# Value tiles between the units of the first head's maxima in a two-layer decoder kernel

## The chip, the cores and the metric

The kernel runs on one core of a Trainium2 chip. The metric is the device time of one execution in microseconds, and smaller is better. The core has five engines that run their own instruction lists and wait for each other by semaphores: TensorE (PE in the profile; its weight loads are PEld), VectorE (DVE), ScalarE (ACT), GpSimd (POOL) and SyncE (SP, which only issues DMAs).

## What is computed

Two decoder layers on x of 2048 tokens by 256, each layer a self attention, a cross attention over a context of 1601 tokens, and a feed-forward part (an fp8 matmul in the first layer; an MLP inside the second self attention and a mixture of experts after it). Every attention has 16 heads of 16 columns. The part that matters here, cut from the reference:

```python
def attention(x, ctx, Wq, Wk, Wv, Wo, ...):      # the same form four times
    q, k, v = split_heads(x @ Wq.T + bq), split_heads(ctx @ Wk.T + bk), split_heads(ctx @ Wv.T + bv)
    scores = einsum('bhqd,bhkd->bhqk', q, k) / sqrt(16)
    scores = where(mask, scores, -inf)           # causal, given mask, causal, none
    attn = softmax(scores, axis=-1)
    return einsum('bhqk,bhkd->bhqd', attn, v).reshape(...) @ Wo.T + bo

x = layernorm(x + attention(x, x, ...))          # layer 0, with rope: the first attention
x = layernorm(x + attention(x, ctx_1024, ...))   # the second
...
x = layernorm(x + self_attention_and_mlp(x))     # layer 1: the third
x = layernorm(x + attention(x, ctx_1024, ...))   # the fourth
```

## The kernel before

The program is a row of phases; `attention_phase` (line 124) is called four times, for the first self attention, the first cross attention, the second self attention and the second cross attention. In the text these are the first to fourth attention. All work in it is written by hand in order, one list per engine, and the order of a list is the order of execution. Nothing is scheduled by a planner.

A phase begins with a front. There TensorE makes two kinds of tiles, in the order of the list `front`:

- **cut tiles** (L477 transposes, L481 products): the queries and keys of 8 heads by up to 512 tokens in fp32. ScalarE (L405, L411) and VectorE (L643 or L646, L653) cut each into three bf16 parts, and SyncE and GpSimd store the parts in HBM in turn (L229). There are 16 cut tiles in each attention.
- **value tiles** (L471): 128 tokens by 256 columns, two fp32 matmuls each, 16 of them in a self attention and 13 in a cross attention (the last has 65 tokens). ScalarE copies each into `values` (L426, raises `v_kept`), and in the second to fourth attention GpSimd adds the bias (L354). The memory of `values` is called `vall` in the profile.

Both kinds go in turn through four PSUM banks, 3 to 6 (`front_bank`). `made(kind, i)` waits until the tile four places earlier has been read.

SyncE loads the parts of a head's queries and keys back as a **stack** of 96 rows (L253 and L254, 12 loads a head), the one of head 0 while the last cut tiles are still being made. VectorE sets some constants behind the cuts (memsets, L746 to L751) and waits for them.

Then come the **maxima**: the softmax needs the maximum of each query's scores. A **unit** (`unit(h, u)`) is one piece of the scores of head h with the queries as rows: 128 queries by up to 512 keys in a self attention, four matmuls side by side (L496), with four more that add the causal mask on the diagonal (L500); by 401 or 398 keys in a cross attention. A self attention has 40 units a head, a cross attention 64. Units go in turn through three PSUM banks, 0 to 2 (`M_BANKS`), and VectorE reduces each to a column (L669, in the second attention L665). With all units of a head reduced, VectorE makes the head's maximum in six small steps (`finish_max`, L677 to L692), which stand between the first six units of the next head, SyncE stores it and loads it back into the stack as three more rows (`place_max`, L263 and L266).

TensorE's list is: all of `front`, the units of head 0, the first `early_units` of head 1, then for each head the scores with the keys as rows (`scores`, L520, with the masks L525 or L528), ScalarE's exponentials of them (L434), and their products with the values (`product`, L548). The units of the next heads are mixed in between. The first `scores(0, 0)` waits for the loaded maxima (`max_in`), for `v_kept` of all value tiles, and where there is a bias for `v_shifted` of all of them.

The order of the front, as it is written:

```python
for kind, i in front:
    if loads and (kind, i) == front[len(work) if work[0][0][0] is None else 0]:
        pe.wait_ge(loaded, 16 * len(loads))
    made(kind, i)
for u in range(nu):
    unit(0, u)
for u in range(early_units):
    unit(1, u)
```

## Time and profile before

| | |
|---|---|
| median of 3 runs | 3324.24 us (3316.51 to 3329.48) |
| the profiled execution | 3327.38 us, of which the span is 3325.6 us |
| TensorE busy | 90% |
| VectorE busy | 71% |
| ScalarE busy | 51% |
| GpSimd busy | 15% |
| mean granted clock of TensorE | 0.936 |

The span runs from the first to the last instruction of the profiled execution. Times of a row are counted from its start. A granted clock of 1.00 is 2.4 GHz, one of 0.50 is 1.2 GHz; a number between them over a window is a mean of the two. In a timeline a row may merge several instructions of a line: its second number is the time from the first one's start to the last one's end. The brackets at a row's end give the idle time ahead of it, and what ended it.

### The profile page before, as it was taken

How to read it: one execution, taken by the hardware profiler on the slowest of the kernel's cores; microseconds unless marked ns; L12 is line 12 of the kernel's file. 1: busy time of each engine (PE TensorE's matmuls, PEld its weight loads, DVE VectorE, ACT ScalarE, POOL GpSimd, SP SyncE). 2: the span in 40 equal slices, each digit the busy share in tenths (PEclk: the TensorE clock that was granted, in tenths of full speed). 3: DMA queues.
4: the chain of work that ended last, by engine and by line, in shares of the span. 5: the costliest groups of instructions: out<-in, count | busy, mean ns of one | idle time of the engine just before them, and what ended most of it. 6: DMA issues, size and time to landing. Idle time of an engine off the chain costs nothing. (4 is left out here: it accounts for less than half of the span.)

```text
span 3325.6 us, 96922 instructions
## 1 busy us (share of the span) xinstructions
PE 2983.0 (90%) x41211; PEld 1713.7 (52%) x41211; DVE 2348.1 (71%) x5743; ACT 1708.3 (51%) x2162; POOL 497.9 (15%) x558
## 2 busy tenths in 40 slices
PE   3199999889999999994699999898999999989996
PEld 1146666554556656653346665465333333356663
DVE  5888888558777777746788887215999999733114
ACT  1146666643565555561347777413377777731221
POOL 3335555011000000000122211001100000001113
PEclk8579999997999999997789999999799999989998
DMA  2134333230011100010311111103011221121112
GB/s 63 50 95 112 107 112 106 63 100 14 21 23 24 23 23 18 21 32 16 100 28 44 38 38 35 49 0 115 25 37 49 71 49 43 30 63 56 46 44 81
DMA packets 127271, 171.79 MB, mean 52 GB/s; under 512 B 45719, under 2 KB 97879, under 8 KB 124983
## 3 DMA queue, kind: packets, MB, share of 16 engines
q1 hardware_dynamic: 116040, 118.83, 13.8%
q0 software_dynamic: 10800, 46.76, 4.4%
q8 instruction: 326, 5.34, 0.7%
q14 instruction: 105, 0.86, 0.1%
HBM read 122.50 MB, written 35.13 MB: 47 GB/s over the span
## 5 line engine op out<-in xcount | busy, mean ns | idle before, releaser
L669 DVE TENSOR_REDUCE mpart<-ps 128x1 f32<-128x512 f32 (+5 forms) x2304 | 1245.4, 589 | 142.9 <-PE ps L496 78.2
L496 PE MATMUL ps<-stack 96*32 96x401 bf16 (+5 forms) x13312 | 1266.7, 355 | 22.2 <-DVE mpart L669 18.0
L520 PE MATMUL ps<-stack 99*32 99x512 bf16 (+3 forms) x11648 | 1137.0, 369 | 40.9 <-ACT xT L434 19.8
L434 ACT ACTIVATE xT<-ps 128x1024 f32<-128x1024 f32 (+3 forms) x800 | 732.2, 938 | 444.4 <-PE ps L520 237.0
L434 ACT ACTIVATE cn<-ps 128x1024 f32<-128x1024 f32 (+4 forms) x800 | 686.8, 870 | 337.2 <-PE ps L520 176.8
L496 PEld LDWEIGHTS ps<-stack 96*32 96x32 bf16 x13312 | 496.6, 96 | 511.7 <-DVE mpart L669 250.2
L665 DVE CUSTOM_DVE_ANT_0 scrap<-ps,arena 128x401 bf16<-128x401 f32 (+1 forms) x1024 | 550.3, 574 | 150.0 <-PE ps L496 125.5
L520 PEld LDWEIGHTS ps<-stack 99*32 99x32 bf16 x11648 | 417.2, 97 | 358.6 <-issue 122.4
L548 PE MATMUL ps<-xT,vall 128*17 128x512 f32 (+4 forms) x3648 | 455.9, 506 | 0.1
L548 PE MATMUL ps<-cn,vall 128*17 128x512 f32 (+3 forms) x3392 | 441.7, 496 | 0.9 <-ACT cn L434 0.5
L528 PE MATMUL ps<-arena,big 128*32 128x512 fp8e4 (+1 forms) x3264 | 360.7, 381 | 0.0
L500 PE MATMUL ps<-upper,ident 128*32 128x128 bf16 x2048 | 216.3, 227 | 0.0
L548 PEld LDWEIGHTS ps<-xT,vall 128*17 128x17 f32 (+1 forms) x3648 | 134.0, 98 | 47.1 <-issue 2.5
L528 PEld LDWEIGHTS ps<-arena,big 128*32 128x32 bf16 (+1 forms) x3264 | 123.7, 98 | 52.6 <-issue 5.0
L548 PEld LDWEIGHTS ps<-cn,vall 128*17 128x17 f32 (+1 forms) x3392 | 126.9, 98 | 43.5 <-ACT cn L434 3.2
L1287 PE MATMUL ps<-arena,vall 128*128 x312 | 146.6, 593 | 0.6 <-ACT vall L1358 0.6
L1517 DVE TENSOR_TENSOR vall<-osb,ps 128x512 f32<-128x512 f32 x39 | 26.8, 687 | 146.2 <-PE ps L1287 146.2
L525 PE MATMUL ps<-lower,ident 128*32 128x128 bf16 x1024 | 122.3, 223 | 0.0
L500 PEld LDWEIGHTS ps<-upper,ident 128*32 128x32 bf16 x2048 | 105.5, 100 | 24.6 <-issue 1.1
L1017 POOL PARTITION_ALL_REDUCE small<-small x1 | 0.4, 371 | 743.3 <-issue 743.3
L1372 ACT ACTIVATE osb<-ps 128x512 f32<-128x512 f32 x39 | 23.3, 598 | 169.8 <-PE ps L1287 169.8
L371 POOL TENSOR_SCALAR arena<-wbuf 128x1601 bf16<-128x1601 int32 x16 | 90.2, 5640 | 81.6 <-DMA wbuf<-in_mask 81.6
(235 smaller groups left out, 2646.4 us busy)
## 6 DMA issues: line engine op xcount, KB each, us to landing
stack<-q_parts SPq DMA_DIRECT2D x384, 64.0 KB, 2.6
wbuf<-in_mask POOLq DMA_DIRECT2D x16, 800.5 KB, 5.5
stack<-k_parts SPq DMA_DIRECT2D x192, 64.0 KB, 2.7
wbuf<-in_maskT POOLq DMA_DIRECT2D x12, 1024.0 KB, 5.4
arena<-in_moe_w SPq DMA_DIRECT2D x19, 512.0 KB, 4.5
stack<-k_parts SPq DMA_DIRECT2D x192, 50.0 KB, 2.3
parts<-osb SPq DMA_DIRECT2D x240, 32.0 KB
q_parts<-parts SPq DMA_DIRECT2D x16, 384.0 KB, 3.1
```

What stands on the lines that cost most here:

```text
L371: chain.link(nc.gpsimd.tensor_scalar(e.mask_add[:, t, :], given[:, 0:S2], 0.0, MASKED, ALU.is_equal, ALU.mult))
L434: nc.scalar.activation(e.prob[tile % P_SLOTS][0:rows, half * HALF + first:(half + 1) * HALF], S_PS(g)[0:rows, first:HALF], ACT.Exp, scale= ...
L496: last = nc.tensor.matmul(bank[quarter(j), 0:w], qs[b][0:KQ, t * P + 32 * j:t * P + 32 * j + 32], ks[b][0:KQ, a:a + w], start=True, stop=n ...
L500: last = nc.tensor.matmul(bank[quarter(j), w - P:w], e.ident16[:, quarter(j)], e.upper16, start=False, stop=True)
L520: last = nc.tensor.matmul(S_PS(g)[quarter(j), lo:hi], ks[b][0:KM, kt * P + 32 * j:kt * P + 32 * j + 32], qs[b][0:KM, half * HALF + lo:half ...
L525: last = nc.tensor.matmul(S_PS(g)[quarter(j), lo:lo + P], e.ident16[:, quarter(j)], e.lower16, start=False, stop=True)
L528: last = nc.tensor.matmul(S_PS(g)[quarter(j), lo:hi], e.big16[0:rows, quarter(j)], e.mask_one[0:rows, kt, half * HALF + lo:half * HALF + h ...
L548: last = nc.tensor.matmul(O_PS[quarter(j, HD + 1), b0 * P:CH], e.values[0:rows, kt, h, :], weights[0:rows, b0:4, j, :], start=(kt == 0), s ...
L665: nc.vector.tensor_tensor_reduce(out=e.scrap[:, g % 4, 0:w], in0=src, in1=e.mask_add[:, t, a:a + w], scale=1.0, scalar=-3.0e38, op0=ALU.ad ...
L669: nc.vector.tensor_reduce(dst, src, AX, ALU.max).then_inc(unit_used, 1)
L1287: last = nc.tensor.matmul(bank, e.pair_xT[i % 2][:, c, :], w, start=(c == 0), stop=(c == NC - 1))
L1517: nc.vector.tensor_tensor(e.pair_h[i % 2], e.gated_s[i % 2], b_bank(i), ALU.mult).then_inc(pair_h, 1)
```

## The change

The loop over `front` on TensorE is split. The cut tiles are made first, as before. The value tiles are no longer made behind them: one is made behind every second or third unit of head 0 in a self attention (16 among 40 units) and behind every fourth or fifth in a cross attention (13 among 64). The last one stands behind the last unit. The wait for the loaded weights (`loads`, in the first attention alone) stays ahead of the first unit.

```diff
-                for kind, i in front:
-                    if loads and (kind, i) == front[len(work) if work[0][0][0] is None else 0]:
-                        pe.wait_ge(loaded, 16 * len(loads))
-                    made(kind, i)
+                turned_front = work[0][0][0] is None
+                if loads and not turned_front:
+                    pe.wait_ge(loaded, 16 * len(loads))
+                for i in range(len(work)):
+                    made("cut", i)
+                if loads and turned_front:
+                    pe.wait_ge(loaded, 16 * len(loads))
+                valued = 0
                 for u in range(nu):
                     unit(0, u)
+                    while valued < nk * (u + 1) // nu:
+                        made("value", valued)
+                        valued += 1
                 for u in range(early_units):
                     unit(1, u)
```

Only TensorE's list changes. The lists of the other four engines are the same, instruction by instruction. Each value tile is two rows of L471 in the list; `x2` counts them.

TensorE in the first attention, from the last cut transposes to unit 4, before. The names: `ps` is PSUM, `arena` holds the queries and keys, `wbuf` the value weights, `xT` the turned x, `stack_304` the stack of head 0, `upper` the causal mask.

```order
L477 MATMUL ps<-ident,arena 128x128 x64
L471 MATMUL ps<-wbuf,xT 128x256 x32
L496 MATMUL ps<-stack_304 32x128 x4
L500 MATMUL ps<-upper,ident 32x128 x4
L496 MATMUL ps<-stack_304 32x256 x4
L500 MATMUL ps<-upper,ident 32x128 x4
L496 MATMUL ps<-stack_304 32x384 x4
L500 MATMUL ps<-upper,ident 32x128 x4
L496 MATMUL ps<-stack_304 32x512 x4
L500 MATMUL ps<-upper,ident 32x128 x4
```

The same place after the change:

```order
L477 MATMUL ps<-ident,arena 128x128 x64
L496 MATMUL ps<-stack_304 32x128 x4
L500 MATMUL ps<-upper,ident 32x128 x4
L496 MATMUL ps<-stack_304 32x256 x4
L500 MATMUL ps<-upper,ident 32x128 x4
L496 MATMUL ps<-stack_304 32x384 x4
L500 MATMUL ps<-upper,ident 32x128 x4
L471 MATMUL ps<-wbuf,xT 128x256 x2
L496 MATMUL ps<-stack_304 32x512 x4
L500 MATMUL ps<-upper,ident 32x128 x4
```

The 32 matmuls of the 16 value tiles are gone from behind the transposes; the first tile stands behind unit 2.

TensorE in the second attention, from the last cut tiles to the first units, before. Here `cn` holds the turned context, which the value tiles and the keys are made from, and a unit is 32x401 x4 or 32x398 x4.

```order
L481 MATMUL ps<-cn,wbuf 128x512 x6
L481 MATMUL ps<-cn,wbuf 128x65 x2
L471 MATMUL ps<-wbuf,cn 128x256 x24
L471 MATMUL ps<-wbuf,cn 65x256 x2
L496 MATMUL ps<-stack_13673 32x401 x12
L496 MATMUL ps<-stack_13673 32x398 x4
```

After the change:

```order
L481 MATMUL ps<-cn,wbuf 128x512 x6
L481 MATMUL ps<-cn,wbuf 128x65 x2
L496 MATMUL ps<-stack_13673 32x401 x12
L496 MATMUL ps<-stack_13673 32x398 x4
L496 MATMUL ps<-stack_13673 32x401 x4
L471 MATMUL ps<-wbuf,cn 128x256 x2
L496 MATMUL ps<-stack_13673 32x401 x8
L496 MATMUL ps<-stack_13673 32x398 x4
L496 MATMUL ps<-stack_13673 32x401 x8
L471 MATMUL ps<-wbuf,cn 128x256 x2
```

The tiles stand five units apart, and no longer between the last cut tile and unit 0.

## Rows read from the trace of the kernel before

**Rows 1.** The page, part 1: busy time, share of the span, instructions.

```profile
PE 2983.0 (90%) x41211; PEld 1713.7 (52%) x41211; DVE 2348.1 (71%) x5743; ACT 1708.3 (51%) x2162; POOL 497.9 (15%) x558
```

**Rows 2.** Timeline, TensorE, first attention: start us, us, engine, line, operation, count.

```profile
172.88 11.56 PE L471 MATMUL ps<-wbuf,xT 128*128 128x256 f32 x52 [1.17 <-DVE parts L643]
185.47 0.70 PE L496 MATMUL ps<-stack 96*32 96x512 bf16 x8
```

**Rows 3.** Timeline, VectorE, first attention.

```profile
181.57 0.48 DVE L751 MEMSET ps<- 128x512 f32 x1
184.79 20.84 DVE L669 TENSOR_REDUCE mpart<-ps 128x1 f32<-128x128 f32 x40 [2.73 <-PE ps L500]
205.67 0.22 DVE L677 TENSOR_REDUCE mfin<-mpart 128x16 f32<-128x64 f32 x1
```

**Rows 4.** Timeline, SyncE's queue and TensorE, first attention; the page, part 6.

```profile
171.88 0.43 SPq L254 DMA_DIRECT2D stack<-q_parts  x1
...
213.19 0.62 PE L520 MATMUL ps<-stack 99*32 99x512 bf16 x4 [0.82 <-DMA stack<-max_parts]
...
stack<-q_parts SPq DMA_DIRECT2D x384, 64.0 KB, 2.6
```

**Rows 5.** Windows: us, TensorE busy (count), granted clock, DMA share, GB/s.

```profile
190.00:192.00 2.00, 1.50 (x20) 0.74 0.00 0
728.00:735.20 7.20, 4.77 (x20) 1.00 0.82 245
746.00:748.00 2.00, 1.45 (x18) 0.84 0.57 116
```

**Rows 6.** Timeline, TensorE and VectorE, second attention.

```profile
743.99 0.70 PE L496 MATMUL ps<-stack 96*32 96x401 bf16 x12
745.16 0.35 PE L496 MATMUL ps<-stack 96*32 96x398 bf16 x4 [0.47 <-DVE mpart L665]
...
742.15 0.48 DVE L751 MEMSET ps<- 128x512 f32 x1
744.52 0.58 DVE L665 CUSTOM_DVE_ANT_0 scrap<-ps,arena 128x401 bf16<-128x401 f32 x1 [1.89 <-PE ps L496]
745.02 0.57 DVE L665 CUSTOM_DVE_ANT_0 scrap<-ps,arena 128x401 bf16<-128x401 f32 x1
...
776.31 0.22 DVE L677 TENSOR_REDUCE mfin<-mpart 128x16 f32<-128x64 f32 x1
```

**Rows 7.** Timeline, VectorE, third attention.

```profile
1657.38 0.48 DVE L751 MEMSET ps<- 128x512 f32 x1
1660.61 20.84 DVE L669 TENSOR_REDUCE mpart<-ps 128x1 f32<-128x128 f32 x40 [2.74 <-PE ps L500]
1681.49 0.22 DVE L677 TENSOR_REDUCE mfin<-mpart 128x16 f32<-128x64 f32 x1
```

**Rows 8.** Timeline, VectorE, fourth attention.

```profile
2324.36 0.48 DVE L751 MEMSET ps<- 128x512 f32 x1
2326.69 30.89 DVE L669 TENSOR_REDUCE mpart<-ps 128x1 f32<-128x401 f32 x64 [1.85 <-PE ps L496]
2357.62 0.22 DVE L677 TENSOR_REDUCE mfin<-mpart 128x16 f32<-128x64 f32 x1
```

**Rows 9.** Windows behind the first scores of the four attentions.

```profile
213.20:221.70 8.50, 8.23 (x88) 0.50 0.31 83
785.30:788.30 3.00, 3.00 (x36) 0.50 0.44 101
1688.80:1696.20 7.40, 7.11 (x64) 0.50 0.36 97
2368.80:2375.50 6.70, 6.43 (x60) 0.50 0.14 35
```

**Rows 10.** Timeline and window, TensorE, first cut tiles of the second attention.

```profile
702.12 9.22 PE L481 MATMUL ps<-xT,wbuf 128*128 128x512 f32 x16 [1.04 <-PEq L240]
...
706.00:708.00 2.00, 2.00 (x5) 0.90 0.00 0
```

## The prediction

> **What bounds the kernel now.** I read the page first: TensorE is busy 90% of the span [rows 1], so outside a few stages whatever delays TensorE delays the end. The diff touches one stage, which occurs four times, once in each attention phase: the value tiles and the maxima of head 0. So I read TensorE's and VectorE's timelines of these four stretches, then the granted clock in them, then what the first scores wait for.
>
> In the first attention the 16 value tiles run on TensorE without a gap until the first unit starts. The row of 52 products gives the price of a tile: the first 51 take 11.56 less the last one's 0.38, so 11.18 / 51 = 0.22 us each at the full clock, and a tile has four in the trace (two matmuls, each recorded as two), 0.87 us [rows 2]. VectorE ends its memsets at 181.57 + 0.48 = 182.05 and idles 2.73 us for the first unit. Then it reduces 40 units in 20.84 us and goes on at 205.67 with the final maximum of head 0 [rows 3]. In this stretch VectorE is the bound and TensorE waits for banks. After it come the final maximum, two copies by SyncE and the first scores, which wait on the copy of the maxima with 0.82 us of idle TensorE [rows 4]. **So the end of VectorE's head 0 is on the path**, and what it moves by, the first scores move by; from there TensorE is dense, and I expect no later stage to give the shift back. The third attention has the same form (1657.86, 1660.61, 1681.49) [rows 7]. The cross attentions have 64 units: memsets end at 742.63, first unit 744.52, head 0 ends 776.31 [rows 6]; and 2324.84, 2326.69, 2357.62 [rows 8].
>
> **Part 1: the value tiles leave the place ahead of unit 0.** Removed there: 58 tiles (16 + 13 + 16 + 13) of 0.87 us. Not all of that was on the path, since VectorE's memsets ran beside them. What VectorE can win is the idle time between its last memset and its first reduction: 2.7, 1.9, 2.7 and 1.9 us, together 9.2 us. For this the stack of head 0 must have arrived by 182.05: its last load was issued at 171.88 and a load of this size lands in 2.6 us [rows 4], so near 175, with 7 us to spare. Units 0 to 2 then stand in their banks when VectorE is ready. After its last cut TensorE now waits for the stack, does three units, and waits again for VectorE: it is nearly idle for 8 to 13 us where it was dense.
>
> **Part 2: the tiles now stand between the units.** The cost is TensorE time in a stretch that VectorE bounded. Constants from the rows: a unit takes TensorE its width at 2.4 GHz, 0.21 us for 512 columns and 0.17 for 401; the rows agree, with two of the one and three of the other in 0.70 us, the last one's way to the bank included [rows 2, 6]. VectorE's pitch is 0.60 for 512, 20.84 / 40 = 0.52 in the mean, 0.50 for the masked 401 (744.52 to 745.02) and 30.89 / 64 = 0.48 for the unmasked [rows 3, 6, 8]. After VectorE is done with a bank TensorE restarts 0.15 us later (745.02 to 745.16) and VectorE gets a unit 0.36 us after its last column has entered (743.99 + 0.17 to 744.52) [rows 6]. The weight load of a tile I cost at nothing, since TensorE's loads run ahead; uncovered at each of the 58 tiles it would be about 0.1 us, so up to 5.8 us, which I keep for the upper end.
>
> Self attention (first and third): 40 units have 17408 columns and 2048 more for the diagonals. Without the first three units 18304 are left, at 2.4 GHz 7.6 us, and 15 tiles of 0.87 are 13.0. That makes 20.6 us of TensorE, with 0.35 before it (first reduction 0.20, restart 0.15), and 0.36 and 0.60 behind it until VectorE is done: 21.9 us. VectorE alone needs 20.9. **TensorE becomes the bound by a little.** Narrow early units do not cover a tile; I put 0.5 us on that.
>
> Cross attention: VectorE needs 31.7 us (second) and 30.9 (fourth). A tile lies between two units in a ring of three banks. From the release of a bank to the next but one unit in VectorE's hands it takes 0.15 + 0.17 + 0.87 + 0.17 + 0.36 = 1.72 us; three reductions cover 1.49 or 1.45. So each of 12 tiles (the 13th stands behind the last unit) costs 0.23 or 0.27: 2.8 and 3.2 us.
>
> **Part 3: the clock.** The granted clock falls from 1.00 to 0.50 (2.4 to 1.2 GHz) in the unit stage of before: the mean of 0.74 over 190 to 192 puts it near 191, 6.6 us after the last value tile, and in the second attention near 747.4, 3.4 us after it [rows 5]. It is then low until 2.9 to 8.5 us after the first scores [rows 9]. Changed, TensorE comes to the interleaved stretch out of a nearly idle time, so I take it to start there at 1.2 GHz. How long? In the second attention's cuts TensorE starts dense at 702.12 and the clock is back near 706.4 (0.90 over 706 to 708): 4.3 us [rows 10]. At half clock TensorE is behind in all four stages and therefore dense, so I take 4.3. In a self attention this loses half of it, 2.1 us. In a cross attention a group of five units and a tile at 1.2 GHz takes 1.73 for the tile, 0.33 + 0.36 + 0.50 + 0.15 until the fourth unit may start, 0.50 and 0.33 for the fourth and fifth: 3.9 us, against 2.7 at full clock; 4.3 us hold 1.1 such groups, so 1.3 us.
>
> The Trainium skill ("TensorE: Matmul & The Clock Gate", section "HAM oscillation — how this bites in real kernels") says that idle stretches between bursts send TensorE back to half rate; that speaks against this change, which puts such a stretch right ahead of TensorE's heaviest work. If the clock were full at once, as the plain reading of the 1.00 in the value stage of before would have it, the sum below would be 6.8 us lower.
>
> **The sum.** First attention: 182.05 + 21.9 + 0.5 + 2.1 = 206.55, was 205.67: +0.9. Third: the same, +0.9. Second: 742.63 + 31.7 + 2.8 + 1.3 = 778.4, was 776.3: +2.1. Fourth: 2324.84 + 30.9 + 3.2 + 1.3 = 2360.2, was 2357.6: +2.6. Together **+6.5 us**. ScalarE and GpSimd keep their orders: the value copies and the bias additions only come later, the last of them some 1.5 us after head 0 ends, while the first scores follow 7.5 us after it in the first attention (205.67 to 213.19). GpSimd's additions now lie beside the reductions; they did so in the third attention already, where 40 reductions took the same 20.84 us as in the first, which has none [rows 3, 7]. So both cost nothing. The profiled execution took 3327.4 us (span 3325.6), the median is 3324.2. By the first the sum is 3334, by the median 3331; I give 3331.
>
> **Rivals.**
> The clock stays at 2.4 GHz beyond the values (faster). The tiles keep TensorE fuller up to the end of head 0, and the first scores might then start at full clock. Before, the first scores ran 8.5, 3.0, 7.4 and 6.7 us at 0.50 [rows 9]: 25.6 us, of which half, 12.8, could come back. Against it: from the end of head 0 to the first scores there are 7.5 us of lone units and waiting in the first attention and 9 in the second (776.31 to 785.3), and before the clock fell 3.4 and 6.6 us after the last tile [rows 5]. It gives 3331 - 13 = 3318; without any cold start as well, 3311. The Trainium skill (same page, "Why this matters for your kernels") advises keeping TensorE continuously busy, which speaks for this one.
>
> The clock stays low or comes and goes while tiles and units alternate (slower). The Trainium skill (same page, "A second HAM failure mode: psum-queue depth-cycling") tells of such a coming and going. As a mechanism of this kernel: TensorE's work of 20.6 us becomes 41.2 at 1.2 GHz, and VectorE starves. All four stages low to the end would give 18.7 twice in the self attentions (182.05 + 41.2 + 1.3 = 224.5), and about 17 in each cross attention (12.8 groups of 3.9 are 50 us, so 742.6 + 50 = 792.6 against 776.3): +71, 3395 us. Against it: in the cuts of the second attention, with TensorE busy 4.77 of 7.20 us, the clock held 1.00 [rows 5], and the interleaved stretch is fuller. Each microsecond at 1.2 GHz beyond 4.3 costs 0.5 us (self) or 0.3 (cross); it takes some 27 us more of low clock to come past 0.5% slower. Halfway, with 10 more in each stage: +16, 3347.
>
> VectorE doesn't start earlier (the change doesn't do what it says). If the first unit were still late for some other reason, say a later stack, the 9.2 us would not be won: 3340. The 7 us to spare speak against it.
>
> No ring waits and no cold start (the gain alone): 2.7 + 1.9 + 2.7 + 1.9 less the 1.0 of TensorE's excess twice: -7, 3317.
>
> **How the numbers follow.** Forecast 0.58, clock kept into the scores 0.12, low clock longer 0.18, no earlier start 0.05, gain alone 0.07. A difference under 0.5% (16.6 us) can hardly be told from no change here: the three runs of before span 13 us. The forecast's own bounds are +0 (weight loads free, quick clock) to +12 (loads uncovered). Taken to the median's own spread and to the halfway case, the range is **3312 to 3350**. Only the low-clock rival beyond its halfway point gives over 0.5% slower, with measuring spread 0.13; faster by over 0.5% needs kept clock and no cold start together, 0.05; the rest, 0.82, is no change that can be told.
>
> **What would show it.** VectorE's first unit of head 0 within 0.2 us of its last memset in all four stages; TensorE's clock at 0.50 at that time and up some 4 us later; head 0 lasting about 24.5 us where it was 20.9 and 35 where it was 31 to 32; waits of VectorE of 0.2 to 0.3 us behind each tile in the cross attentions; first scores again at 0.50. I am wrong if the clock is at 1.00 when VectorE begins, if it falls again between tiles, or if head 0 ends earlier than before.

## The result: 3352.9 us, slower by 0.9%, and the profile after

The changed kernel takes 3352.89 us by its median (3342.1 to 3359.5), the kernel before 3321.91 (3316.5 to 3329.5) beside it. The ratio is 1.0092, with an interval of 1.0066 to 1.0118: slower by 22 to 39 us. The forecast was 3331, with 3350 as the upper bound. The profiled execution took 3352.9 us (span 3351.1), 25.5 more than that of before (span 3325.6). This is the execution that can be taken apart.

The page, part 1, of the changed kernel, which answers to [rows 1]:

```profile
PE 2958.7 (88%) x41211; PEld 1686.4 (50%) x41211; DVE 2360.3 (70%) x5743; ACT 1708.9 (51%) x2162; POOL 499.1 (15%) x558
```

TensorE is busy for 24 us less in a longer span: in the four stages more of its work is done at the full clock, and more of its time is waiting.

The timeline of TensorE in the first attention, changed kernel (start us, us, engine, line, operation, count, idle time before and who ended it), answering to [rows 2, 4]. Lines from L578 on stand seven lower than in the kernel before (L669 is now L676, L751 is L758):

```profile
177.17 0.30 PE L496 MATMUL ps<-stack 96*32 96x128 bf16 x4 [9.28 <-DMA stack<-q_parts]
...
178.25 2.07 PE L471 MATMUL ps<-wbuf,xT 128*128 128x256 f32 x4
183.98 0.62 PE L496 MATMUL ps<-stack 96*32 96x512 bf16 x4 [3.65 <-DVE mpart L676]
...
219.68 0.62 PE L520 MATMUL ps<-stack 99*32 99x512 bf16 x4 [0.77 <-DMA stack<-max_parts]
```

After its last cut TensorE waits 9.3 us for the stack of head 0, makes three units and a tile (2.07 us, at the low clock), and waits 3.65 us for VectorE.

The timelines of VectorE in the four attentions: last reset of a bank (the memset of `ps`), first unit, final maximum of head 0. They answer to [rows 3, 6, 7, 8]:

```profile
183.11 0.48 DVE L758 MEMSET ps<- 128x512 f32 x1
183.63 2.41 DVE L676 TENSOR_REDUCE mpart<-ps 128x1 f32<-128x128 f32 x5
187.53 1.45 DVE L676 TENSOR_REDUCE mpart<-ps 128x1 f32<-128x128 f32 x3 [1.48 <-PE ps L500]
...
212.10 0.22 DVE L684 TENSOR_REDUCE mfin<-mpart 128x16 f32<-128x64 f32 x1
...
754.08 0.48 DVE L758 MEMSET ps<- 128x512 f32 x1
754.60 0.58 DVE L672 CUSTOM_DVE_ANT_0 scrap<-ps,arena 128x401 bf16<-128x401 f32 x1
...
792.62 0.22 DVE L684 TENSOR_REDUCE mfin<-mpart 128x16 f32<-128x64 f32 x1
...
1673.33 0.48 DVE L758 MEMSET ps<- 128x512 f32 x1
1673.85 0.29 DVE L676 TENSOR_REDUCE mpart<-ps 128x1 f32<-128x128 f32 x1
...
1701.37 0.22 DVE L684 TENSOR_REDUCE mfin<-mpart 128x16 f32<-128x64 f32 x1
...
2344.07 0.48 DVE L758 MEMSET ps<- 128x512 f32 x1
2344.59 0.58 DVE L676 TENSOR_REDUCE mpart<-ps 128x1 f32<-128x401 f32 x1
...
2382.45 0.22 DVE L684 TENSOR_REDUCE mfin<-mpart 128x16 f32<-128x64 f32 x1
```

VectorE now starts within 0.04 us of its last reset in all four: the gain of part 1 is there. But from the end of that reset to the final maximum it takes 28.5, 38.1, 27.6 and 37.9 us, where it took 23.6, 33.7, 23.6 and 32.8: **18.3 us more in the four stages**. From the final maximum to the first scores come 0.9 us more in all (0.06, 0.30, 0.22, 0.35).

Windows of the changed kernel (us, TensorE busy, granted clock, DMA share, GB/s), from VectorE's first unit on, and around the first scores of the first attention, answering to [rows 5, 9]:

```profile
183.60:189.60 6.00, 5.62 (x40) 0.50 0.49 124
189.60:212.10 22.50, 22.50 (x230) 1.00 0.01 2
754.60:759.60 5.00, 4.33 (x28) 0.50 0.50 118
759.60:792.60 33.00, 27.69 (x276) 1.00 0.02 7
1673.80:1677.80 4.00, 3.61 (x28) 0.50 0.57 136
2344.60:2350.20 5.60, 4.96 (x32) 0.50 0.53 139
216.90:227.20 10.30, 9.26 (x96) 0.50 0.32 82
```

The clock is at 1.2 GHz when the stage starts and goes up after 4.0 to 6.0 us; then TensorE is busy without a gap in the self attentions. It falls again behind the final maximum (at 216.9 us in the first attention, the first scores start at 219.68), so the first scores of all four attentions are at 1.2 GHz again.

**Where the 25.5 us of span lie:** 18.3 in the stages, 0.9 behind them, 5.9 in the head loop of the first attention (first score to last product: 451.9 us, was 445.9), 0.4 in all the rest (1.5 ahead of the first stage, -1.1 elsewhere). The head loops of the other attentions are equal within 1 us.

### The profile page after: what moved, and what is told of

It reads as the page before. It is cut to its first block and busy times, and to the rows that moved or that the text cites. A ratio compares the mean times of both kernels' runs of the same rounds, so it can differ in the third digit from the quotient of the medians.

```text
span 3351.1 us, 96922 instructions
## 1 busy us (share of the span) xinstructions
PE 2958.7 (88%) x41211; PEld 1686.4 (50%) x41211; DVE 2360.3 (70%) x5743; ACT 1708.9 (51%) x2162; POOL 499.1 (15%) x558
## 5 line engine op out<-in xcount | busy, mean ns | idle before, releaser
L676 DVE TENSOR_REDUCE mpart<-ps 128x1 f32<-128x512 f32 (+5 forms) x2304 | 1252.3, 590 | 152.2 <-PE ps L496 91.7
L496 PE MATMUL ps<-stack 96*32 96x401 bf16 (+5 forms) x13312 | 1225.9, 346 | 81.8 <-DVE mpart L676 37.1
L496 PEld LDWEIGHTS ps<-stack 96*32 96x32 bf16 x13312 | 482.9, 96 | 549.1 <-DVE mpart L676 235.4
L520 PEld LDWEIGHTS ps<-stack 99*32 99x32 bf16 x11648 | 410.4, 97 | 363.6 <-issue 124.6
L528 PEld LDWEIGHTS ps<-arena,big 128*32 128x32 bf16 (+1 forms) x3264 | 116.6, 98 | 57.4 <-issue 4.3
```

The lines of the kernel that those rows point to most:

```text
L496: last = nc.tensor.matmul(bank[quarter(j), 0:w], qs[b][0:KQ, t * P + 32 * j:t * P + 32 * j + 32], ks[b][0:KQ, a:a + w], start=True, stop=n ...
L520: last = nc.tensor.matmul(S_PS(g)[quarter(j), lo:hi], ks[b][0:KM, kt * P + 32 * j:kt * P + 32 * j + 32], qs[b][0:KM, half * HALF + lo:half ...
L528: last = nc.tensor.matmul(S_PS(g)[quarter(j), lo:hi], e.big16[0:rows, quarter(j)], e.mask_one[0:rows, kt, half * HALF + lo:half * HALF + h ...
L676: nc.vector.tensor_reduce(dst, src, AX, ALU.max).then_inc(unit_used, 1)
```

## The experiments

**Is it the clock?** The changed kernel with products without use that keep TensorE busy while it waits ahead of unit 0 and behind unit 2.

```diff
+                for i in range(warm_a):
+                    nc.tensor.matmul(e.ps[:, 2, 0:D], v_source[:, 0, 0:P], v_weights[:, 0, :], start=True, stop=True)
                 for u in range(nu):
                     unit(0, u)
+                    if u == 2:
+                        pe.wait_ge(rest_made, len(work))
+                        for i in range(warm_b):
+                            nc.tensor.matmul(e.ps[:, S_FIRST + 3, 0:D], v_source[:, 0, 0:P], v_weights[:, 0, :],
+                                             start=True, stop=True)
```

> The changed kernel with TensorE kept busy where it idled: 16, 12 or 18 fp32 products of 128 by 256 behind the last cut tile (first attention, third, cross), written to the bank of unit 2 and overwritten by it, and 11 or 10 more between unit 2 and the end of VectorE's memsets. All results stay the same. Theory 'cold clock' (the stage is long because TensorE comes to it at 1.2 GHz): from the last memset to the end of head 0 the stages fall from 28.5, 38.1, 27.6 and 37.9 us nearly back to the 23.6, 33.7, 23.6 and 32.8 of before, and the kernel gains 15 us or more on the changed one. Theory 'switch' (a value tile between units costs TensorE 1.18 us where a tile in a row cost 0.87): the granted clock is 1.00 at VectorE's first unit, but each stage gets shorter by only 1 to 2.5 us, to about 26, 36.8, 26 and 36.6, and the kernel stays 13 to 25 us above the one before.

Measured: 3331.28 us (3327.2 to 3336.1), ratio to the kernel before 1.0020 (1.0008 to 1.0032). Windows from the last reset to the final maximum, this kernel:

```profile
182.00:208.00 26.00, 25.57 (x268) 1.00 0.11 30
732.10:768.90 36.80, 30.67 (x305) 1.00 0.10 27
1650.60:1676.50 25.90, 25.59 (x268) 1.00 0.10 26
2320.70:2357.10 36.40, 30.12 (x300) 1.00 0.10 28
```

The clock is full throughout, and the stages take 26.0, 36.8, 26.0 and 36.4 us: 6.9 less than in the changed kernel, still 11.4 more than before. These are the stage times that the 'switch' theory gave. So the cold clock costs 6.9 us in this pair of profiles and the interleaving itself takes the rest. The time of the whole kernel is not as that theory had it, which was 13 to 25 us above the kernel before: the medians are 7.2 apart (3324.06 for the kernel before, beside it). This kernel's median is 21.6 us under the changed one's, which is more than 6.9: in the profiles another 15.6 lie in the first attention's loop, 436.2 us here. That loop is taken up below.

**What does a tile between units cost?** TensorE's timeline in the second attention, changed kernel, at the full clock:

```profile
765.18 0.85 PE L496 MATMUL ps<-stack 96*32 96x401 bf16 x8 [0.34 <-DVE mpart L672]
765.96 1.13 PE L471 MATMUL ps<-wbuf,cn 128*128 128x256 f32 x4
767.02 0.70 PE L496 MATMUL ps<-stack 96*32 96x401 bf16 x12
```

From the start of the tile to the next unit it is 767.02 - 765.96 = 1.06 us, where four products in a dense row take 0.87 [rows 2]. The tile itself starts 0.28 us after the last unit (765.68 in the trace), whose 398 columns take 0.17 at 2.4 GHz. That is 0.30 us per tile on top of 0.87: 0.10 ahead of the tile and 0.20 from its start on. Of these, 0.10 lies between the tile's first and second product (0.32 us from start to start, 0.215 in a dense row) and 0.10 between its last product and the next unit (0.31). All 49 full tiles that TensorE makes between units at the full clock show the same 1.06 us in this trace. The Trainium skill ("TensorE: Matmul & The Clock Gate", Part 3, "The mechanism") says that a weight load overlaps matmuls in flight only on other row groups; the tile's weights take all 128 rows of the array and the units' weights 96 of the same rows, and the trace agrees in so far as neither change is hidden. Two kernels try the reading. In one, tiles stand two and two, so that there are half as many changes:

```diff
-                    while valued < nk * (u + 1) // nu:
+                    while valued + 2 <= nk * (u + 1) // nu or (u == nu - 1 and valued < nk):
                         made("value", valued)
                         valued += 1
+                        if valued < nk:
+                            made("value", valued)
+                            valued += 1
```

> The changed kernel with the value tiles two and two: a pair behind every fifth unit in a self attention, behind every ninth or tenth in a cross attention. Theory 'switch': there are half as many changes from units to a tile and back, each worth 0.31 us of TensorE. Where TensorE is the bound (self attentions) the stage gets shorter by up to 7 times 0.31, 2 us, less what VectorE waits for a pair of 2.05 us. Where VectorE is the bound (cross) the ring of three banks covers 1.49 us, and a pair takes 0.14 + 0.29 + 1.93 + 0.41 = 2.77 from the release of a bank: 1.28 us of wait for each of 6 pairs, 7.7 us in place of 12 times 0.41 = 4.9, so the cross stages get longer by 2 to 3 us. Theory 'cold clock': no difference in either. Total by 'switch': within 4 us of the changed kernel.

Measured: 3372.06 us (3366.6 to 3374.3), ratio 1.0141 (1.0118 to 1.0165); worse than either kernel, and neither expectation had that. Its stages take 32.3, 45.4, 31.5 and 43.3 us, 20.4 more than in the changed kernel. TensorE in the second attention of this kernel, a pair and the units behind it:

```profile
771.72 1.34 PE L496 MATMUL ps<-stack 96*32 96x401 bf16 x12
772.99 1.99 PE L471 MATMUL ps<-wbuf,cn 128*128 128x256 f32 x8
774.92 0.70 PE L496 MATMUL ps<-stack 96*32 96x401 bf16 x12
775.97 3.33 PE L496 MATMUL ps<-stack 96*32 96x398 bf16 x28 [0.35 <-DVE mpart L675]
```

The pair takes 774.92 - 772.99 = 1.93 us to the next unit, 0.19 less than two single tiles (2.12): what lies behind a tile's start is paid once per pair, as read. But three banks of units cover one tile at most, and a pair uncovers the whole second one. In the self attentions, where the clock is as in the changed kernel, the stages are 3.7 and 3.9 us longer by this. From pair to pair, ten units apart, it is 6.22 us at the full clock, where two tiles five units apart make 5.77 in the changed kernel. And in the cross attentions the granted clock comes and goes (0.70 over 748 to 765, 0.89 over 765 to 790), which the changed kernel did not show.

In the other, the tile's products are made from the upper halves of the fp32 words, as bf16 (the value tiles are then less exact; that is the part of the computation that changes):

```diff
-                            last = nc.tensor.matmul(bank[0:n, 0:D], v_source[:, c, a:a + n], v_weights[:, c, :],
-                                                    start=(c == 0), stop=(c == NC - 1))
+                            short = (v_source[:, c, a:a + n].bitcast(BF16).rearrange("p (n two) -> p n two", two=2)[:, :, 1],
+                                     v_weights[:, c, :].bitcast(BF16).rearrange("p (n two) -> p n two", two=2)[:, :, 1])
+                            last = nc.tensor.matmul(bank[0:n, 0:D], *short, start=(c == 0), stop=(c == NC - 1))
```

> The changed kernel with the value tiles computed in bf16 (the upper halves of the fp32 numbers, read with a stride of two), so the values are less exact; nothing else is changed. Two matmuls a tile, each one pass. It shows what the 0.31 us are that a tile costs beyond its columns when it stands between units. Theory 'weight load' (the first load of 128 by 128 fp32 weights, 0.19 us, can't run ahead of the units): with a shorter bf16 load the time beyond the columns falls to 0.1 to 0.2 us. Theory 'changeover' (TensorE must let the units drain on both sides, whatever is loaded): it stays at 0.3. Stages get shorter in any case, by 13 to 16 times 0.65 us of TensorE where that is the bound.

Measured: 3317.85 us in one run. TensorE in the first attention of this kernel, at the full clock:

```profile
195.04 0.40 PE L497 MATMUL ps<-stack 96*32 96x512 bf16 x4 [0.20 <-DVE mpart L677]
195.37 0.40 PE L473 MATMUL ps<-wbuf,xT 128*128 128x256 bf16 x2
195.70 0.40 PE L497 MATMUL ps<-stack 96*32 96x512 bf16 x4
```

The tile takes 0.33 us to the next unit, where its columns take 0.215, and it starts 0.33 us after the unit ahead of it, whose 512 columns take the same: 0.23 us of change is left of 0.30. A load of its weights is recorded with 0.10 us, where one of fp32 has 0.19. What shrank is the part inside the tile, from 0.10 to 0.02; the 0.10 or so ahead of the tile and behind it stayed. So the type of the weights is the smaller part of the price, and neither theory holds alone: the load accounts for some 0.07 us, and what makes the other 0.2 (a load that cannot start earlier, or products that must drain) no run here shows. In the cross attentions the clock never rose during the units of head 0 in this kernel. Windows over both stages:

```profile
733.80:768.40 34.60, 33.63 (x278) 0.50 0.10 27
2312.60:2346.80 34.20, 33.42 (x278) 0.50 0.09 25
```

TensorE is recorded as 97 to 98% busy there and stays at 1.2 GHz; the stages are still 3.4 and 3.6 us shorter than in the changed kernel.

**Is it better to move only a few tiles, late?** All but three (self) or two (cross) tiles ahead, two in the second half of the units, and the third of a self attention behind the last one.

```diff
-                valued = 0
+                back = 3 if causal else 2
+                for t in range(nk - back):
+                    made("value", t)
+                valued = nk - back
                 for u in range(nu):
                     unit(0, u)
-                    while valued < nk * (u + 1) // nu:
+                    if u >= nu // 2 and u % 8 == 0 and valued < nk:
```

> Most value tiles ahead of unit 0 again, as before; only the last 3 (self) or 2 (cross) are made between later units of head 0. So TensorE is dense until its first unit, and it reaches unit 0 just as VectorE ends its memsets. Theory 'switch': VectorE wins 2.3 to 2.7 us (self) and 1.5 to 1.8 (cross) at the start and pays about 0.2 to 0.4 for each tile behind it: stages of about 21.7, 32.6, 21.7 and 31.7 us from the last memset to the end of head 0, together 6 us less than before; kernel 3 to 8 us below the one before. Theory 'later loss' (the change costs something in the head loops because the values come late): the stages shorten but the kernel is not faster than before.

Measured: 3328.48 us (3319.7 to 3340.9), ratio 1.0012 (0.9998 to 1.0026): no gain, a miss. The stages take 24.0, 34.0, 23.1 and 34.4 us, 1.8 more than before in all. VectorE starts early, but some 3 to 7 us into the units the clock is down again, as it was in the kernel before, and six of the eight tiles between units start at 1.2 GHz, where a tile takes 2.01 us to the next unit and not 1.06. With single tiles eight units apart the clock also comes and goes: in the first attention it is low from 190.3 us, full from 197.1, low from 200.5 and full from 204.0. VectorE in the first attention of this kernel:

```profile
193.82 2.47 DVE L682 TENSOR_REDUCE mpart<-ps 128x1 f32<-128x512 f32 x4
197.56 2.08 DVE L682 TENSOR_REDUCE mpart<-ps 128x1 f32<-128x512 f32 x4 [1.27 <-PE ps L496]
```

The tile at 195.10 costs it 1.27 us. Tiles that seem free in a stretch that VectorE bounds are not, if the clock is at 1.2 GHz when they come.

## The experiments on the first attention's head loop

No instruction of this loop differs between the two kernels, and it took 445.9 us before, 451.9 after and 436.2 in the warm kernel. GpSimd loads and converts the masks of the second attention beside it. VectorE and GpSimd at 571 us, kernel before:

```profile
570.87 5.60 DVE L686 CAST mneg<-mrest 128x16 bf16<-128x16 f32 x1
...
570.80 5.62 POOL L371 TENSOR_SCALAR arena<-wbuf 128x1601 bf16<-128x1601 int32 x1 [4.27 <-DMA wbuf<-in_mask]
...
576.54 0.53 PE L496 MATMUL ps<-stack 96*32 96x512 bf16 x4 [4.11 <-DVE mpart L669]
```

A cast that takes 0.165 us by its median takes 5.60, until GpSimd's conversion ends, and TensorE stands still for 4.11 us. The Trainium skill ("SBUF — State Buffer", "Who interferes with whom") says that VectorE's casts and tensor-scalar steps can need the port pair that it shares with GpSimd, and that whoever comes second is blocked for the whole instruction. I took scalar-tensor-tensor to be free of this and put it in place of the three steps, in the kernel before and in the changed one:

```diff
-                        made = nc.vector.tensor_copy(middle, e.mrest)
+                        made = nc.vector.scalar_tensor_tensor(out=middle, in0=e.mrest, scalar=0.0, in1=e.mrest,
+                                                              op0=ALU.mult, op1=ALU.add)
```

> The kernel before, with three of the six small steps of each head's maximum written as scalar_tensor_tensor (-2m + m, 0*m + m, 1*m - middle), which give the same numbers. In the traces so far one of these steps sometimes takes 2.4 to 5.6 us in place of 0.17 in the first attention's head loop, always beside a mask conversion of 5.6 us on GpSimd; the two scalar_tensor_tensor steps that are there already never do. Theory 'collision' (a cast or tensor_scalar of VectorE waits until GpSimd's long operation is over, and how many do depends on how heads and mask conversions happen to be aligned): no step over 1 us in this loop, the loop takes about 430 us where it took 446, and the kernel gains 10 to 16 us. Theory 'chance of the clock' (the lost time is the clock's alone): the loop keeps its 436 to 452 us.

> The changed kernel with the same three steps rewritten. With the collisions gone from both, the difference between this and b_stt is the price of the change itself. Theory 'switch and cold clock' (all of it lies in the four stages): this is 18 to 20 us above b_stt (0.54 to 0.60%), the four stages 28.5, 38.1, 27.6 and 38 to 39 us again, the first attention's loop within 2 us of b_stt's. Theory 'later loss': 25 to 31 us above b_stt, with the rest in the head loops.

Measured: 3325.54 us (ratio 0.9994, 0.9979 to 1.0009) and 3349.32 (1.0068, 1.0046 to 1.0091). The theory of the free step fell: the new steps are held too, up to 3.7 us. The same section of that page says that an instruction with two inputs in SBUF contends with a GpSimd instruction that reads SBUF, which is what I had built. What this pair still gives is its difference, 23.8 us between the medians, and 22.7 in the profiles: 19.0 in the stages, 1.1 behind them, 4.1 in the loop, -1.5 elsewhere.

Next, GpSimd's conversions in pieces of 256 columns:

```diff
-                        chain.link(nc.gpsimd.tensor_scalar(e.mask_add[:, t, :], given[:, 0:S2], 0.0, MASKED,
-                                                           ALU.is_equal, ALU.mult))
+                        for s in range(0, S2, PIECE):
+                            part = slice(s, min(s + PIECE, S2))
+                            chain.link(nc.gpsimd.tensor_scalar(e.mask_add[:, t, part], given[:, part], 0.0, MASKED,
+                                                               ALU.is_equal, ALU.mult))
```

> The kernel before, with GpSimd's 29 mask conversions in the first attention (5.4 and 5.6 us each) cut into pieces of 256 columns, some 0.7 to 0.8 us each; nothing else changes. Open is why the first attention's loop, from the first score to the last product, takes 446 us in the profile of the kernel before, 452 in that of the changed one, 436 in those of the warm and the paired kernel, where no instruction of it differs. Theory 1 (length of the block): a small VectorE step that falls beside a conversion is held until that conversion ends, so how much a kernel loses is luck of alignment times 5.6 us; with pieces it can be held for one piece, no step of the reciprocal's kind lasts over 1.1 us, the loop takes 434 to 438 us, and the time falls by 8 to 12 us against the kernel before, to about 3314. Theory 2 (the steps are slowed as long as GpSimd works, however it is cut): steps of 2 to 5 us stay, the loop takes 442 to 450, and the time stays within 3 us of the kernel before.

> The changed kernel with the same pieces on GpSimd. Theory 1: the first attention's loop takes the same 434 to 438 us as in the kernel before with pieces, so the difference between these two is that of the four stages and the waits behind them alone, 19 to 20 us by the profiles (18.3 + 0.9), and the changed kernel with pieces lies at about 3334, some 14 to 18 us under the changed kernel. Theory 2: its loop stays at 447 to 452 us and the difference between the two stays at 24 to 31 us. A third way, that the change itself slows the first attention's loop through TensorE: both kernels have short steps, and this one's loop is still 3 to 6 us longer.

Measured: 3329.73 us (ratio 1.0008, 0.9993 to 1.0023) and 3348.64 (1.0066, 1.0040 to 1.0092). In the first no such step of VectorE lasts over 0.4 us, and its loop takes 448.9. So a step is held no longer than one piece, as theory 1 had it, but the loop doesn't gain by that, and as explanations of its length both theories are out. In the second some still last up to 1.8 us, beside GpSimd's casts of 1.9 us, which were left whole; TensorE waits 1.3 us for VectorE in its loop of 445.0. TensorE's waits in the loop (in total, times, longest), first the kernel before, then that with pieces:

```profile
PE ps L496 <- DVE mpart L669: 13.2, 6, 4.1
PE ps L520 <- ACT xT L434: 7.4, 18, 0.8
PE ps L520 <- DMA stack<-max_parts: 6.8, 7, 2.2
```

```profile
PE ps L527 <- DMA stack<-max_parts: 19.1, 12, 3.0
```

The waits for VectorE are gone and those for the transfer of the maxima have taken their place, 19.1 us where they were 6.8. To part the causes, three kernels in which the masks' place is filled with zeros (the second attention then masks nothing): the two orders without any mask work, and that of before with the loads and no conversion.

```diff
-                        nc.gpsimd.dma_start(given[:, 0:S2], e.d["mask"][t * P:(t + 1) * P, :]).then_inc(mask_in, 16)
-                        staged += 1
-                        pool.wait_ge(mask_in, 16 * staged)
-                        chain.link(nc.gpsimd.tensor_scalar(e.mask_add[:, t, :], given[:, 0:S2], 0.0, MASKED,
-                                                           ALU.is_equal, ALU.mult))
+                        chain.link(nc.gpsimd.memset(e.mask_add[:, t, :].bitcast(BF16), 0.0))
```

> The kernel before, in which GpSimd neither loads nor converts the masks in the first attention but fills their place with zeros (so the second attention masks nothing; its work is the same). By the traces so far the first attention's loop lasts 410 to 413 us (the third attention's has 411 and no masks beside it), plus TensorE's waits over 0.15 us there (20 to 32 us), plus half the time at the low clock (7 to 24 us). Theory L (the masks make all of that): the loop takes 412 to 418 us in this kernel, and its time is about 30 us under the kernel before, near 3293. Rival: the waits on the rows of maxima belong to the loop and stay, 18 us as with conversions in pieces: 430 us and more, 3310.

> The changed kernel without masks in the first attention, likewise (the second attention masks nothing). It measures the change by itself. If the change costs only in the four stages and the waits behind them, the difference to the kernel before without masks is the 19.2 us of the profiles (18.3 + 0.9), within 18 to 21. If it also slows the first attention's loop by what TensorE or VectorE do there, the difference is 24 to 31, and the loop is longer by 3 us and more than in its partner.

> The kernel before, in which GpSimd loads the masks as ever but converts nothing (their place is filled with zeros, the second attention masks nothing). It parts the two ways in which the masks cost. If the late rows of maxima (waits of the scores on that transfer: 6 us with long conversions, 17 to 18 with conversions in pieces) come from the mask transfers themselves, they are here too, at 10 us and more, and the loop takes 425 to 440 us. If they come from conversions that hold VectorE or GpSimd, they are gone and the loop takes 412 to 418 us as without masks.

Measured: 3304.71 us, 3326.64 us, and 3324.62 us in one run. The loop takes 420.3, 421.9 and 442.1 us. Windows over it and the waits on the maxima, first without masks, then with the loads alone, both in the old order:

```profile
213.10:633.40 420.30, 410.12 (x8716) 0.99 0.16 40
...
PE ps L510 <- DMA stack<-max_parts: 0.9, 2, 0.6
```

```profile
214.10:656.20 442.10, 418.12 (x8716) 0.97 0.35 97
...
PE ps L520 <- DMA stack<-max_parts: 16.0, 7, 3.9
```

So **the masks' transfers alone are enough for 22 of the 26 us** by which the loop of the kernel before is longer: the small transfers of a head's maxima come late, and TensorE waits. The trace shows the lateness itself. Without masks the load of the maxima (L266) lands 1.6 to 1.8 us after its issue and the second store ahead of it (L263) after 1.9 to 2.5. With the mask loads alone, four such loads take 3.0 to 5.3 us and three such stores 4.0 to 5.9, at six heads in all, and behind these TensorE waits 1.0 to 3.9 us. Behind the three longest waits the clock is down for 3.4 or 6.8 us. This is one run, and without conversions its mask transfers follow each other sooner than in the kernel before (all are issued by 445 us), so it says what they can do and not how the 26 us are shared out there. The conversions, which looked like the culprit, mostly trade one wait for the other.

And the change by itself, with all this away, costs 21.9 us between the medians. The two profiled executions are 28.6 apart (that of the changed order was the slowest of its ten, the other the second fastest of its six): 21.8 in the stages, 1.3 behind them, 1.7 in the loop and 3.8 elsewhere, 1.5 of it ahead of the first stage.

The same two kernels once more, for a second profile each:

> The changed kernel once more, for its trace: which of the differences between the two traces repeat. If the 5.9 us that the first attention's head loop was longer (451.9 against 446.0 us from the first scores to the last product) belong to the change, they are here again; if they are chance, that is another count of windows in which the granted clock was 0.50 in this loop, the loop comes back to 446 to 449 us. The stage times 28.5, 38.1, 27.6 and 37.9 us should repeat within 1 us, up to the moment at which the clock rises.

> The kernel before once more, for a second profile. The length of the first attention's loop has been taken from one profile of it (445.9 us), and lay at 443 to 449.5 in the five other kernels of the old order and at 436 to 452 in those of the new. If it is luck of the execution, it moves by several us here, and the part of the 31 us that the four stages do not explain is not the change's; if it returns within 1 us, the loop's length belongs to the kernel's timing, and the change's 449 and 452 in two profiles are its own.

Measured: 3352.57 and 3330.93 us; the loop 449.1 us (was 451.9) and 444.2 us (was 445.9). It moves by 2 to 3 us from one execution to the next.

## The experiments toward a faster kernel

Five to seven tiles ahead of the units, so that TensorE is warm and the stack has arrived; the rest behind every fourth or fifth unit; and the rows of ones set by GpSimd at the start of the attention, so that VectorE is free earlier. It also has the three scalar-tensor-tensor steps.

```diff
+                ahead_n = 7 if turned_front else 5 if causal else 6
+                for t in range(ahead_n):
+                    made("value", t)
+                valued = ahead_n
                 for u in range(nu):
                     unit(0, u)
+                    while valued < nk and (u % 4 == 3 if causal else u % 5 == 4):
+                        made("value", valued)
+                        valued += 1
...
```

> A version that follows from what was found. VectorE's three long memsets of the stacks go to GpSimd at the phase's start, so VectorE is ready when the stack arrives, 4 to 6 us earlier. 7, 5 or 6 value tiles (first attention, third, cross) fill TensorE's wait for the stack and bring it there warm; the other 9, 11 and 7 stand behind every fourth unit (self) or every fifth (cross), dense enough to hold the clock. The three small steps are rewritten. Expected by 'switch and cold clock': the head 0 of each stage starts 7 us earlier than before (self) or 6 (cross) and lasts about 2 to 3 us longer: 4 times 3 to 4 us won, 12 to 16 us below b_stt, 25 us or so below the kernel before. If TensorE's tiles cost more than that, no gain over b_stt.

> The kernel before (all value tiles ahead of the units) with one difference: GpSimd sets the rows of ones, at the start of the attention, in place of VectorE behind the value tiles. It separates what the best kernel owes to an earlier free VectorE from what it owes to the moved tiles. VectorE's first unit then waits for TensorE alone: 2.3 us less at the start of the self attentions (last reset of a bank to first unit, 2.7 in the kernel before) and about 1.9 us less in the cross ones if that is so, and the time is 4 to 8 us under the kernel before. If the rows of ones were hidden anyway behind the tiles that TensorE makes (the first unit comes 0.3 us behind TensorE's last tile in the kernel before), nothing changes, within 2 us. I hold the second likelier for all four, since there the unit ends the wait and not VectorE: then the gain of the best kernel (12 us) is that of the tiles that moved.

Measured: **3313.98 us** (3303.3 to 3323.9), ratio 0.9963 (0.9948 to 0.9979), and 3324.36 with the rows of ones alone, ratio 0.9999 (0.9981 to 1.0017). The second does nothing, as I had held likelier, since there the first unit ends VectorE's wait. The first is faster than both kernels by a little (0.2 to 0.5% under the one before; its profiled execution, 3323.9 us, was the slowest of twelve): from the last product of one attention to the final maximum of the next it saves 2.5 to 4.6 us, and its own stage starts warm. Windows from VectorE's first unit to the final maximum, first and second attention:

```profile
177.90:203.10 25.20, 21.10 (x264) 1.00 0.20 61
739.60:774.20 34.60, 29.86 (x288) 0.84 0.15 41
```

The same with conversions in pieces and plain steps:

> The kernel with five to seven tiles ahead of the units, the rest behind every fourth or fifth, and the rows of ones set by GpSimd, now with VectorE's plain steps again (the fused ones had brought nothing) and with GpSimd's conversions in pieces. Its loop in the first attention took 449.5 us in its profile. Theory 1: that falls to 434 to 438, and the time to some 3302, 12 us under the same kernel without pieces. Theory 2: 3314, as without pieces.

Measured: 3315.25 us, ratio 0.9956 (0.9941 to 0.9972): no difference, as with the pieces above. Last, the masks loaded and converted in halves, with the order of before and with that of the best kernel:

```diff
+                        for part in (slice(0, 801), slice(801, S2)):
+                            staged_in(P, "mask", t * P, part)
+                            chain.link(nc.gpsimd.tensor_scalar(e.mask_add[:, t, part], given[:, part], 0.0, MASKED,
+                                                               ALU.is_equal, ALU.mult))
```

> The kernel before with the masks of the first attention handled in halves: GpSimd loads half the columns of a mask tile (some 400 to 512 KB), converts them (half of 5.4 or 5.6 us), then the other half. In the runs so far the masks' transfers alone made the loop 442 us where it is 420 without masks, by waits of the scores on the rows of maxima (16 us) and the low clock behind each; conversions then trade such waits for waits on VectorE. If the length of one transfer and of one conversion is what hurts, both fall: TensorE's waits from 29 us to 15 to 20, the loop to 430 to 436, and the time by 8 to 14 us, to about 3312. If it is the bytes moved, or that GpSimd is busy, that counts, the loop stays at 440 to 450 and the time within 4 us of the kernel before. As the pieces of conversions alone brought nothing, I hold the two about equal.

> The kernel with five to seven tiles ahead of the units and the rest behind every fourth or fifth, with the masks in halves. Its stages should be as in the kernel with masks whole (25.3, 34.6, 25.3 and 34.1 us from VectorE's first unit to the end of head 0), 12 us under the kernel before in all; with the loop at 430 to 436 the time is about 3300, with the loop unchanged about 3313.

Measured: 3335.63 us (ratio 1.0030, 1.0014 to 1.0045) and 3320.35 (0.9991, 0.9978 to 1.0003). The loop fell to 426.9 and 427.5 us, further than I expected, and the time did not. TensorE and GpSimd after the loop, kernel before with halves:

```profile
695.69 2.89 POOL L377 TENSOR_SCALAR arena<-wbuf 128x800 bf16<-128x800 int32 x1 [2.94 <-DMA wbuf<-in_mask]
...
708.23 8.89 PE L487 MATMUL ps<-xT,wbuf 128*128 128x512 f32 x16 [22.43 <-PEq L240]
```

GpSimd is done with the masks only at 698.6 us (587.1 before). The weights of the next attention are loaded behind that, and TensorE waits 22.4 us for them at its first cuts (1.0 before [rows 10]). The gain of 19 us is given back at one place, in a wait that begins 44 us behind the loop's end.

## Why the prediction was wrong, by its own steps

**Part 1, the earlier start: right.** Forecast 9.2 us, measured 9.1: VectorE's idle time of 2.7, 1.9, 2.7 and 1.9 us is 0.04 in each stage.

**Part 2, the tiles between the units: right in mechanism, too small in size, and the step that failed.** I set the tile at 0.87 us and the change from units to tile and back at nothing, with 0.1 us as the upper bound. It is 0.30. Measured without the clock (warm kernel, first unit to final maximum, less the same stretch of before): 5.0, 4.9, 5.0 and 5.5 us. The forecast was 1.5, 2.8, 1.5 and 3.2. That is 20.5 against 9.0: **11.5 us missing in one term**. In a self attention it is 15 tiles of 0.30, all on a TensorE that was the bound already (21.9 + 4.5 is 26.4, measured 25.9, so the 0.5 for narrow units wasn't needed); in a cross attention 12 waits of 0.41 and 0.45 where I had 0.23 and 0.27. There only 0.18 of the 0.30 shows, so the chain of 1.72 us was some 0.12 too long in its other terms. The trace of before had a third of the price, and I read past it. TensorE's last products and first units in the second attention, kernel before:

```profile
743.25 0.81 PE L471 MATMUL ps<-wbuf,cn 128*65 128x256 f32 x3
743.99 0.35 PE L496 MATMUL ps<-stack 96*32 96x401 bf16 x2
```

Three products that end after 0.81 us, 0.38 of them the last one's, start 0.215 apart, the last at 743.68; the first unit follows at 743.99, 0.31 behind it and not 0.215, with no wait shown. That is the 0.10 behind a tile; the parts ahead of it and inside it have no counterpart there. I bounded the weight load by the load of a unit's 32 columns; the tile's is one of 128 (0.19 us each in the changed kernel).

**Part 3, the clock: right in mechanism, and in size with some luck.** Forecast 6.8 us in all, measured 6.9 in the profile of the changed kernel. The low stretch was 4.0 to 6.0 us long where I took 4.3. It varies: the four stages together are 18.3 us longer than before in this profile, 19.0 with the other VectorE steps, and 20 to 22 in the second profile and those with pieces and without masks, with low stretches of up to 9.6 us and the cross stages at 38 or 39 us by when the clock rises. Against the warm kernel those four profiles give 7.6 to 10.6 us in place of the 6.9.

**The sum.** -9.1 + 20.5 + 6.9 = 18.3, the measured difference of the stages. With the waits behind them it is 19.2; I had 6.5. Two smaller slips change nothing: with the clock low to the end the stages give 18.8 and 16.3 us more, so +70 and not +71, and to come past 0.5% by the low clock it takes some 25 us and not 27.

**"From there TensorE is dense, and I expect no later stage to give the shift back": true for three loops.** The first attention's loop is not dense: it holds 29 us in which TensorE stands still, and this part comes and goes with the masks' work. In the profiles the changed kernel's is 5.9 and 3.1 us longer than the first one of before, and 7.6 and 4.8 longer than the second. In four pairs of the two orders, the medians differ by 31.0 (as they are), 23.8 (other VectorE steps), 18.9 (pieces) and 21.9 us (no masks); only the last is free of the masks in this loop. In the five profiles of the new order (two as it is, one of each variant) the stages and the waits behind them are 19 to 23 us longer than in the old one. So some 19 to 23 us are the change's own and shown. The other 8 to 12 of the 31 are in part the loop's (3 to 8 in the profiles) and in part scatter. Tiles between the units do not lengthen the loop by themselves: it took 436.2, 437.1 and 436.4 us in the warm kernel, with pairs and with bf16 tiles, less than in any kernel of the old order with its masks as they were (443.0 to 445.9). Whether the changed kernel's loop is longer by when its heads meet the masks, or whether these executions were unlucky, stays open.

**The rivals.** The clock rose during the units but fell again before the first scores, which ran at 0.50 as before, so the faster one is out. "Low clock longer" did not come to the end of a stage in the changed kernel, and the clock did not fall between its tiles; its coming and going did happen, in the kernel with pairs and in the one with few late tiles. The 3347 of its halfway case was near the result for another reason. The earlier start was real, so "no earlier start" is out, and the ring waits and the cold start both came, so "the gain alone" is too.

**Signs that I had named.** First unit within 0.2 us, clock 0.50 at that time and up after some 4 us, first scores at 0.50: all as said. Head 0 lasting 24.5 and 35 us: it was 28.5 and 38. Waits of 0.2 to 0.3 us behind each cross tile: 0.32 on VectorE and 0.41 in the period. These two would have shown the mis-sized term at a glance.

## What to carry to other kernels

Price an interleaved tile by its changes as well as its columns: look for a place in the trace where the two kinds already alternate, and if there is none, put the full weight load in the sum and not only in the range (here it is 0.19 us, and the price was 0.30). Work moved beside a bound of another engine is free only as far as the ring of banks covers one piece of it at the clock that it will meet, so keep enough dense work ahead to start warm, and do not place two pieces together where the ring covers one. A stall that is removed uncovers the next one (VectorE's hold, then the late transfer, then the late prefetch): follow the time to the end of the kernel before calling it won.

## What the runs showed of the hardware that I had not expected

Changing between units of 32 output columns and an fp32 tile of 128 costs TensorE 0.30 us for the way there and back at 2.4 GHz: 0.10 ahead of the tile, 0.10 between its first and second product, 0.10 behind it; in bf16 it is 0.23. TensorE stayed at 1.2 GHz for 34 us in both cross attentions while recorded as 97 to 98% busy with units and bf16 tiles (one run), and rose to 2.4 GHz after 5 to 10 us with fp32 tiles in the same places (five profiles). VectorE's steps of 0.165 us last up to 5.6 us beside GpSimd's tensor-scalar, and scalar-tensor-tensor with two inputs in SBUF up to 3.7. Beside transfers of 800 to 1024 KB on GpSimd's queue a small load on SyncE's landed up to 5.3 us after its issue (1.6 to 1.8 without them), and TensorE waited up to 3.9 us for it; with the transfers in halves, up to 1.6.
